# W1 and Wo loaded and split during the last batch of the first attention, and the opening units in another order

## What is computed

```python
x = x + _L0_attn_a_ref(_layernorm(x), ...)   # 8 heads, 128 wide, relative positions
x = x + _L0_ffn_ref(_layernorm(x), ...)      # 8 experts, all computed
x = x + _L0_attn_b_ref(_layernorm(x), ...)   # 16 heads, 8 wide, causal
x = x + _L0_ffn_ref(_layernorm(x), ...)
# in the FFN, for each expert e:
h = jnp.einsum('btd,hd->bth', x, W1[e]) + b1[e]
a, b = jnp.split(h, 2, axis=-1)
eo = jnp.einsum('bth,dh->btd', a * jax.nn.sigmoid(b), Wo) + bo
out = out + eo * comb[..., e:e + 1]          # comb: weights of the two best experts
```

## Time and profile before

| | us |
|---|---|
| median of 3 runs | 2921.26 |
| lowest and highest | 2916.53 and 2924.25 |
| the profiled execution | 2921.59 |
| its span | 2919.9 |
| TensorE busy | 2631.4 (90%) |
| VectorE busy | 2041.6 (70%) |
| ScalarE busy | 1656.7 (57%) |
| GpSimd busy | 355.0 (12%) |

### The profile page before, as it was taken

How to read it: one execution, slowest core, us unless ns; L and a number is a source line. 1 busy time by engine, 2 the same in 40 slices (tenths; PEclk the granted TensorE clock), 3 DMA queues, 4 the chain that set the end, 5 groups by cost and what they waited for, 6 DMA issues and landing times.

```text
span 2919.9 us, 45160 instructions
## 1 busy us (share of the span) xinstructions
PE 2631.4 (90%) x14496; PEld 2047.8 (70%) x14496; DVE 2041.6 (70%) x5231; ACT 1656.7 (57%) x3430; POOL 355.0 (12%) x782
## 2 busy tenths in 40 slices
PE   2899999999999999999997079988998989998998
PEld 1688788888888888888886067765555555554777
DVE  3576776767767677677664078869777776773887
ACT  2566666666666666666664044544666656565454
POOL 0000000000000000000000123321221221222344
PEclk9999999999999999999999589978999999999999
DMA  2655556566655566556663100000000000000000
GB/s 84 206 203 205 183 200 209 200 214 207 211 205 201 205 214 214 205 195 205 214 208 110 51 6 1 1 1 1 1 1 1 1 1 1 1 1 1 9 8 15
DMA packets 98467, 321.63 MB, mean 110 GB/s; under 512 B 11556, under 2 KB 25508, under 8 KB 98020
## 3 DMA queue, kind: packets, MB, share of 16 engines
q1 hardware_dynamic: 98234, 318.74, 31.9%
HBM read 158.53 MB, written 157.29 MB: 108 GB/s over the span
## 4 chain that ended last, share of the span: by engine, by line
PE 77%; DVE 11%; ACT 5%; SPq 3%; issue 3%; DMA 1%; POOL 0%; DVEq 0%; ACTq 0%; POOLq 0%
PE ps L238 7%; PE ps L240 7%; PE ps L239 7%; PE ps L608 7%; PE ps L583 5%; PE ps L582 5%; PE ps L721 4%; PE ps L759 4%; PE ps L621 4%; PE ps L623 4%; PE ps L622 4%; PE ps L653 4%; PE ps L741 4%; PE ps L654 4%; PE ps L655 4%
## 5 line engine op out<-in xcount | busy, mean ns | idle before, releaser
L874 ACT ACTIVATE a_Ph<-ps 128x512 fp32r<-128x512 f32 x512 | 305.9, 597 | 474.5 <-PE ps L608 474.4
L1177 DVE CUSTOM_DVE_ANT_0 a_sp<-ps,a_sp 128x1024 f32<-128x1024 f32 x256 | 313.3, 1224 | 184.8 <-PE ps L240 178.9
L952 ACT ACTIVATE r_P<-ps 128x512 f32<-128x512 f32 (+3 forms) x768 | 327.7, 491 | 187.5 <-PE ps L741 183.2
L1183 DVE TENSOR_TENSOR a_Pl<-ps,a_Ph 128x512 fp32r<-128x512 f32 x512 | 349.3, 682 | 10.1 <-ACT a_Ph L874 9.8
L582 PE MATMUL ps<-a_fa,a_ua 128*128 128x384 f32 (+2 forms) x960 | 327.2, 353 | 5.0 <-DMA a_ub<-a_ua 2.6
L903 ACT ACTIVATE r_y<-ps 128x256 f32<-128x256 f32 x512 | 194.4, 385 | 220.9 <-PE ps L655 215.0
L867 ACT ACTIVATE a_sp<-a_sp,a_nm 128x1024 f32<-128x1024 f32 x256 | 295.0, 1152 | 29.4 <-DVE a_nm L1177 29.3
L608 PE MATMUL ps<-ident,a_sp 128*128 128x128 f32 x2048 | 309.0, 273 | 0.0
L653 PE MATMUL ps<-r_Wh,p_xh 128*128 128x512 f32 x512 | 223.0, 436 | 92.1 <-DVE r_Wl L1212 44.6
L721 PE MATMUL ps<-r_K,r_Q 128*128 128x512 f32 (+3 forms) x768 | 281.9, 402 | 18.0 <-DVE r_mx L1339 12.6
L608 PEld LDWEIGHTS ps<-ident,a_sp 128*128 128x128 f32 x2048 | 250.7, 141 | 61.6 <-issue 0.4
(11 more groups left out here) (203 smaller groups left out, 5631.0 us busy)
## 6 DMA issues: line engine op xcount, KB each, us to landing
scr<-a_rt SPq DMA_DIRECT2D x256, 576.0 KB, 3.1
a_sp<-scr SPq DMA_DIRECT2D x256, 512.0 KB, 4.4
a_wc<-wsp SPq DMA_DIRECT2D x24, 512.0 KB, 5.5
wsp<-a_wc SPq DMA_DIRECT2D x8, 512.0 KB, 4.6
a_ub<-a_ua SPq DMA_DIRECT2D x64, 44.0 KB
x<-in_q SPq DMA_DIRECT2D x4, 512.0 KB, 15.9
wst<-in_w1t SPq DMA_DIRECT2D x8, 256.0 KB
out<-x SPq DMA_DIRECT2D x4, 512.0 KB, 3.2
```

The costliest lines, as they stand in the source:

```text
L952: e.activation(self.P[:, pt, off:512], ps[:, bank, off:512], ACT.Exp).then_inc(S["b_exp"], 1)
L1177: e.tensor_tensor_reduce(out=w, in0=ps[:, 2:4, :].rearrange("p a n -> p (a n)"), in1=w, scale=-1.0, scalar=3e38, op0=ALU.add, op1=ALU.min, ...
L1183: e.tensor_tensor(self.Pl[:, n % 3, :], ps[:, 4 + n % 2, :], self.Ph[:, n % 3, :].bitcast(F32), ALU.subtract).then_inc(S["p_lo"], 1)
```

## The change

It has these parts:

- W1's high part, half of its low part, and both parts of Wo get memory of their own (the other half of the low part takes the place of a tile of batches 0 and 2). Two staging buffers, `w1st` and `w1r`, hold a piece each.
- The units ("w1", 0) to ("w1", 8) stand at the end of steps 212, 216, ... 244 of plan_a. For piece k, SP issues its loads, GpSimd subtracts (now for all eight), ScalarE rounds and VectorE subtracts, all in this unit. The loads of piece k use buffer k % 2 and wait for the low part of piece k - 2. The last unit is Wo. What stood for this behind the first attention goes.
- SP issues the weights of head 0 ahead of x, and the loads of x for batches 1 to 3 are issued by ScalarE at the end of steps 4, 12 and 20 ("x_load").
- In the opening, the mix of head 0 comes first, its product in the middle of the layer norm, the rounding of the tables ("cut") and the rest of them ("table") apart, and the multiplication by the mask on GpSimd. Mix and prod of head 1 and x_bias go to the end of steps 0 and 1, the split of the gate weights ("route") to step 26.
- The mask of the second attention, `maskq`, is made by GpSimd behind the first attention, ahead of clearing K.
- TensorE no longer waits for first_attention_done ahead of the FFN; the banks' own semaphores stand for it.

```diff
-    p = splits(0)(0, 6) + [("x_bias", 0), ("table",), ("mix", 0), ("load", 1), ("prod", 0, 7)]
-    p += [("u", 0, 0, 2), ("u", 0, 1, 3), ("copy", 0), ("g", 0, 4)]
+    ln = splits(0)(0, 6)
+    p = [("mix", 0), ("load", 1)] + ln[:4] + [("prod", 0, 7)] + ln[4:] + [("cut",)]
+    p += [("u", 0, 0, 2), ("u", 0, 1, 3), ("copy", 0), ("table",), ("g", 0, 4)]
     for t in range(3):
         p += [("r", t, 0), ("r", t, 1), ("r", t, 2), ("rout", t)]
         if t:
             p.append(("rin", t - 1))
-    p += [("u", 1, 0, 5), ("u", 1, 1, 6), ("copy", 1), ("mix", 1), ("load", 2), ("prod", 1, 7)]
-    extra = {}
+    p += [("u", 1, 0, 5), ("u", 1, 1, 6), ("copy", 1)]
+    extra = {0: [("mix", 1), ("load", 2), ("x_bias", 0)], 1: [("prod", 1, 7)], 26: [("route",)]}
+    for b in range(1, B):
+        extra.setdefault(8 * b - 4, []).append(("x_load", b))
+    for k in range(E + 1):
+        extra.setdefault(64 * (B - 1) + 20 + 4 * k, []).append(("w1", k))
...
+        self.Wh, self.Wl = keep("w1h", [128, E, 512], F32R), keep("w1l", [128, E // 2, 512], F32R)
+        self.nat0 = keep("nat0", [128, 2, 8, 128], F32R)
+        late = self.nat0[:, :, :, :].rearrange("p a k n -> p (a k n)").rearrange("p (k n) -> p k n", n=512)
+        self.w1l = [self.Wl[:, k, :] for k in range(E // 2)] + [late[:, k, :] for k in range(E // 2)]
+        self.oh, self.ol = keep("woh", [128, 2, 128], F32R), keep("wol", [128, 2, 128], F32R)
...
+            self.w1st, self.w1r = sb("w1st", [128, 2, 512]), sb("w1r", [128, 2, 512])
...
+        weight_loads(0)
         e.dma_start(self.x[:, 0:8, :], xin[:, 0:8, :]).then_inc(self.d_x[0], 16)
-        weight_loads(0)
         e.dma_start(self.bias[:, :, :], dr["bias_a"].rearrange("d (a h) -> d a h", a=2)).then_inc(S["d_bias"], 16)
         e.dma_start(self.f0[:, :], bass.AP(dr["feat0"].tensor, 0, [[0, 128], [1, 96]])).then_inc(S["d_f0"], 16)
         e.dma_start(self.tmask[:, :], dr["tmask"]).then_inc(S["d_tmask"], 16)
         e.dma_start(self.raw[0], dr["feat_a"]).then_inc(S["d_tab"], 16)
         e.dma_start(self.raw[1], dr["feat_b"]).then_inc(S["d_tab"], 16)
-        for b in range(1, B):
...
+            elif u[0] == "w1":
+                k = u[1]
+                if k == 0:
+                    e.wait_ge(S["prod_mm"], H)
+                if k >= 2:
+                    e.wait_ge(S["w1_lo"], k - 1)
+                if k < E:
+                    e.dma_start(self.w1st[:, k % 2, :], w1[:, k, :]).then_inc(self.d_w1[k], 16)
+                    bottom_row(self.w1r[:, k % 2, :], "w1r", self.d_w1[k], slice(512 * k, 512 * k + 512))
+                else:
+                    e.dma_start(self.w1st[:, k % 2, 0:256].rearrange("p (k d) -> p k d", k=2),
+                                dr["wo_f"].rearrange("(k p) d -> p k d", p=128)).then_inc(S["d_wo"], 16)
...
-        w1 = dr["w1t"].rearrange("d (e h) -> d e h", e=E)
-        for k in range(E):
-            e.dma_start(self.w1st[:, k, :], w1[:, k, :]).then_inc(self.d_w1[k], 16)
-            bottom_row(self.w1r[:, k, :], "w1r", self.d_w1[k], slice(512 * k, 512 * k + 512))
-        e.dma_start(self.ost, dr["wo_f"].rearrange("(k p) d -> p k d", p=128)).then_inc(S["d_wo"], 16)
...
+        e.wait_ge(S["d_tmask"], 16)
+        for k, n in enumerate((128, NFB)):
+            e.wait_ge(S["tab_hi"], k + 1)
+            e.tensor_scalar(self.raw[k], self.raw[k], self.tmask[0:n, 2 * k + 1:2 * k + 2], None, ALU.mult).then_inc(
+                S["tab_cut"], 1)
+        for k in range(E):
+            st = self.w1st[:, k % 2, :]
+            e.wait_ge(self.d_w1[k], 48)
+            e.tensor_tensor(st, st, self.w1r[:, k % 2, :], ALU.subtract).then_inc(S["w1_sub"], 1)
+
         self.first_attention_done(e)
-        for k in range(0, E, 2):
-            e.wait_ge(self.d_w1[k], 48)
-            e.tensor_tensor(self.w1st[:, k, :], self.w1st[:, k, :], self.w1r[:, k, :], ALU.subtract).then_inc(S["w1_even"], 1)
+        e.memset(self.maskq[:, :], 0.0).then_inc(S["const"], 1)
+        e.wait_ge(S["const"], 4)
+        e.affine_select(out=self.maskq[:, 384:512], in_=self.maskq[:, 384:512], compare_op=ALU.is_ge, fill=NEG,
+                        **cond).then_inc(S["const"], 1)
         e.memset(self.K[:, :, :, :].bitcast(F32), 0.0).then_inc(S["b_kzero"], 1)
...
+        free[2] = free[3] = S["s_add"], NTI
+        free[4] = free[5] = S["p_lo"], 8 * NQ
         free[6] = S["o_lo"], NQ
 
     def tensor_ffn(self, e, f):
         S, ps, free = self.S, self.ps, self.bank_free
-        if f == 0:
-            self.first_attention_done(e)
...
+            elif u[0] == "x_load":
+                ns = slice(8 * u[1], 8 * u[1] + 8)
+                e.dma_start(self.x[:, ns, :], xin[:, ns, :]).then_inc(self.d_x[u[1]], 16)
+            elif u[0] == "route":
+                e.wait_ge(S["wg_diff"], 1)
+                e.activation(self.wgh[:, :], self.wgs[:, :], ACT.Copy).then_inc(S["wg_hi"], 1)
+            elif u[0] == "w1":
+                k = u[1]
+                if k < E:
+                    e.wait_ge(S["w1_sub"], k + 1)
+                    e.activation(self.Wh[:, k, :], self.w1st[:, k % 2, :], ACT.Copy).then_inc(S["w1_hi"], 1)
+                else:
+                    e.wait_ge(S["d_wo"], 16)
+                    e.activation(self.oh[:, :, :].rearrange("p k d -> p (k d)"), self.w1st[:, k % 2, 0:256],
+                                 ACT.Copy).then_inc(S["wo_hi"], 1)
+            elif u[0] == "cut":
...
+            elif u[0] == "route":
+                e.wait_ge(S["d_wg"], 16)
+                e.wait_ge(S["d_wgr"], 32)
+                e.tensor_tensor(self.wgs[:, :], self.wgs[:, :], self.wgr[:, :], ALU.subtract).then_inc(S["wg_diff"], 1)
+                e.wait_ge(S["wg_hi"], 1)
+                e.tensor_tensor(self.wgl[:, :], self.wgs[:, :], self.wgh[:, :].bitcast(F32), ALU.subtract).then_inc(S["wg_lo"], 1)
+            elif u[0] == "w1":
+                k = u[1]
+                if k == E // 2:
+                    e.wait_ge(S["pv_mm"], 128 * (B - 1))
+                if k < E:
+                    e.wait_ge(S["w1_hi"], k + 1)
+                    e.tensor_tensor(self.w1l[k], self.w1st[:, k % 2, :], self.Wh[:, k, :].bitcast(F32),
+                                    ALU.subtract).then_inc(S["w1_lo"], 1)
+                else:
+                    e.wait_ge(S["wo_hi"], 1)
+                    e.tensor_tensor(self.ol[:, :, :].rearrange("p k d -> p (k d)"), self.w1st[:, k % 2, 0:256],
+                                    self.oh[:, :, :].rearrange("p k d -> p (k d)").bitcast(F32),
+                                    ALU.subtract).then_inc(S["wo_lo"], 1)
             elif u[0] == "table":
-                e.wait_ge(S["d_tab"], 32)
-                e.wait_ge(S["d_tmask"], 16)
                 for k, n in enumerate((128, NFB)):
-                    e.wait_ge(S["tab_hi"], k + 1)
-                    self.step(e.tensor_scalar(self.raw[k], self.raw[k], self.tmask[0:n, 2 * k + 1:2 * k + 2], None, ALU.mult))
-                    e.wait_ge(S["dve_step"], self.steps)
+                    e.wait_ge(S["tab_cut"], k + 1)
...
-            for k in range(E):
-                if k % 2:
-                    e.wait_ge(self.d_w1[k], 48)
-                    e.tensor_tensor(self.w1st[:, k, :], self.w1st[:, k, :], self.w1r[:, k, :],
-                                    ALU.subtract).then_inc(S["w1_odd"], 1)
-                e.wait_ge(S["w1_hi"], k + 1)
-                e.tensor_tensor(self.Wl[:, k, :], self.w1st[:, k, :], self.Wh[:, k, :].bitcast(F32),
-                                ALU.subtract).then_inc(S["w1_lo"], 1)
-            e.wait_ge(S["wo_hi"], 1)
-            e.tensor_tensor(self.ol[:, :, :], self.ost, self.oh[:, :, :].bitcast(F32), ALU.subtract).then_inc(S["wo_lo"], 1)
...
-                    if m == 0:
-                        e.wait_ge(S["wo_lo"], 1)```

The order of the instructions, as the two programs give it. ScalarE before, behind the step-212 eviction of the last "r" (L859 evicts r, L874 makes a_Ph, L867 is the exponential):

```order
L874 ACTIVATE a_Ph<-ps 128x512 [waits pv_mm,t_mm]
L859 ACTIVATE a_rt<-ps 128x384 [waits r_mm]
L874 ACTIVATE a_Ph<-ps 128x512 [waits pv_mm,t_mm]
L859 ACTIVATE a_rt<-ps 128x384 [waits d_rout2,r_mm]
L867 ACTIVATE a_sp,a_ls<-a_sp,a_nm 128x1024 [waits s_add]
L874 ACTIVATE a_Ph<-ps 128x512 [waits pv_mm,t_mm]
```

65 lines of the change are left out of this document (23 added, 42 removed).

## The result

| us | before | after |
|---|---|---|
| median (4 runs of each) | 2920.03 | 2952.19 |
| lowest and highest | 2916.53 and 2924.25 | 2947.46 and 2957.38 |
| the profiled execution | 2921.59 | 2947.46 |
| its span | 2919.9 | 2945.7 |
| TensorE busy | 2631.4 | 2638.2 |

The change makes the kernel slower: 1.0112 times before's time, 95% interval 1.01 to 1.0125. The two profiles are 25.8 us apart and the medians 32: the profiled execution of after is the fastest of its four. What follows explains the 25.8.

What follows compares the result with a forecast made beforehand. TensorE was taken to have no slack in the first attention and to be nearly idle at its ends. Terms -88.7 (end), -32.3 (opening), +1.5 (x loads), +134.4 (pieces), +3.0 (Wo) gave +17.9 on 2921.6: 2939 us, range 2900 to 2960.

Steps and rivals of the forecast that it cites:

- opening, with the loads of x: Start of the kernel: reordered opening saves 32.3 us (bounds 28 to 37); loads of x on ScalarE's queue cost 1.5.
- eight pieces: W1 splits in the first attention: each piece stalls 16.8 us (bounds 13.9 and 19.5), +134.4 us for eight.
- Wo: Step 244: loading Wo costs 3 us, bounds 0 and 5.
- seam, up to the first merged tile: End of the first attention: FFN's first gate 91.3 us sooner, 0.6 and 2.0 given back, -88.7 us.
- order argument: W1 pieces: load and use stand in one step, so two buffers fetch nothing early and ScalarE waits.
- the price of GpSimd's multiplication: Opening: multiplying a table by the mask on GpSimd takes 1.7 us by its memset, 5.0 by its subtraction.
- The second term: Opening: mix and product 1 moved to steps 0 and 1, -7.5 us, with +3 given back (bounds 0 and 5).
- The term of 1.5: Steps 4, 12 and 20: loads of x may delay a rotated tile, +1.5 us, bounds 0 and 6.
- (a): W1 pieces: stalls cheaper, 15 us a piece, cancelling the gain, about 2925 us; chance 0.22.
- (b): W1 pieces: TensorE runs further ahead in the wait, 12.4 us a piece, 2904 us; chance 0.14.
- (d): Slow clock stays 6 us after each stall and x loads block ScalarE, 20 us a piece, 2965 us; chance 0.04.
- (c): W1 loads hidden if SP reaches a piece a step or more before ScalarE, 2802 us; chance 0.05.

Runs made afterwards that it cites:

- early2: The changed kernel with the loads of each piece of W1 issued two steps earlier: 2875.35 us, ratio 0.9859.
- early4: The changed kernel with the loads of each piece of W1 issued four steps earlier: 2869.73 us, ratio 0.9851.
- early4_split: The changed kernel with the loads four steps earlier and the repeated row split into transfers over 112 and 15 partitions: 2799.78 us, ratio 0.9596.
- poolq: The changed kernel with the pieces' loads issued by GpSimd on its own queue, two pieces ahead, repeated row not split: 2804.06 us, ratio 0.9608.
- row_on_act: The changed kernel with loads four steps early, the unsplit repeated row issued by ScalarE and the rest by SP: 2822.25 us, ratio 0.9677.

## Why the prediction was right in its sign, and where its terms were off

| term | forecast | measured in the profile |
|---|---|---|
| opening, with the loads of x | -32.3 + 1.5 | -28.9 |
| eight pieces | +134.4 | +146.3 |
| Wo | +3.0 | +4.7 |
| on the way to the last addition | 0 | +1.3 |
| seam, up to the first merged tile | -88.7 | -89.2 |
| behind it | 0 | -8.4 |
| sum | +17.9 | +25.8 |

The order argument held: with loads and uses in one step, two buffers fetched nothing ahead, ScalarE waited for GpSimd at each of eight pieces, and the gain at the seam was more than paid for. The forecast was 2939, the median 2952, the profiled execution 2947.5. That the sum came out as near as 7.9 us is in part luck: the terms up to the first merged tile were 16.3 us too low together, and 8.4 came back in stages for which the forecast had nothing.

- **The seam** was sized right in both its parts: the first gate 91.7 us sooner (forecast 91.3), 2.6 given back behind GpSimd's clearing of K (forecast 2.6).
- **The opening.** The first r was forecast at 38.0 with bounds 36.1 and 40.0, and ran at 41.03. The step that failed is the price of GpSimd's multiplication: 5.44 us a table, above the bound of 5.0 that was taken from a subtraction of two tiles, so a one-operand pass was no cheaper per element than a two-operand one. GpSimd's second table was ready at 38.3, which with a VectorE pass of 2.35 gives 40.65. Its effect on VectorE beside it, 5.80 for 2.35 us, was not in the sum at all, but fell mostly into that wait and cost only the last 0.3 us. By the Trainium skill ("GPSIMD Engine Reference", Engine selection) the tables would have been ready near 36.1; the measurement decides against it here. The second term was right: 7.3 us for mix and product 1 (forecast 7.5), and 3.3 given back on balance (forecast 3).
- **The loads of x** cost nothing visible: no distance is lost in after at steps 4, 12 and 20. In early2, early4, early4_split, poolq and row_on_act 0.8 to 1.1 us go at step 4, but step 4's minimum starts there (77.1 to 78.3 us) before the first of these loads is issued (78.4 to 79.6), so they are not its cause. The term of 1.5 should have been nothing. With step 4 and a clock of 0.83 between 84 and 94 us (1.00 in after), the same opening was worth 25.4 to 26.5 us at step 8 in these five kernels: 28.8 is not a constant of the change.
- **A piece** was forecast at 16.8 and cost 18.29, inside its bounds of 13.9 and 19.5. Two sub-steps were short. From the first issue to use it took 16.36 and not 14.7: by difference to the 13.42 of before, what stood ahead in SP's queue cost 2.9 us and not 1.3. And behind TensorE's idle time (15.47 us here, 15.3 on average) came 2.9 more and not 1.3: four microseconds at the lower clock, with a further 0.59 us of waiting for the low half of P, which stood behind the piece and the minimum on VectorE. The wait that stopped TensorE first was also another one than named: the r matmul waiting for ScalarE's eviction, not the pv matmul waiting for the low half.
- **Wo** cost 4.7 us, near its upper bound of 5.
- **Behind the first tile** the forecast had nothing, and 8.4 us came back. From the first merged tile to the end, before and then after:

```profile
1694.08:2919.87 1225.79, 1114.77 (x5879) 740.05 (x5877) 930.71 (x2862) 678.90 (x1549) 338.66 (x764) 0.94 0.01 3
...
1728.26:2945.72 1217.46, 1105.83 (x5876) 734.27 (x5876) 929.32 (x2861) 678.14 (x1547) 338.65 (x764) 0.95 0.01 3
```

TensorE does the same work in 8.9 us less busy time and is idle for as long as before, 111 us, so the gain goes with the granted clock. The change did not aim at it: the same stages took 1217 to 1223 us in the other kernels. That the clock is the cause is read from such rows only; no run tested it.

**The rivals.** (a) and (b) needed pieces of 15 us and less. (d) came nearest in its price, 20, though by the queue and the clock and not by ScalarE's blocked issue: ScalarE's issues of x took about 0.4 us each. (c) said 2802 if the loads were hidden; early4_split hides them and takes 2799.8. Its terms met the forecast as a sum, not singly: the opening was 5.4 us worse, and 4.8 us came back behind the first merged tile. What its condition lacked is that asking a step or more ahead is not enough: early4 does so and takes 2869.7, since the repeated row then holds up the tiles of the same queue. The prediction took 13.4 us from issue to use from a row and never asked why 254 KB should take that long when 512 KB land in 4.4. That question would have led to the transfer that cost before 68 us all along.

## What to carry to other kernels

Two buffers hide a load only if the issuing engine reaches the issue before the users reach the use; where all engines walk one list, give the load a place of its own, some steps ahead. Then look at what stands behind it in its queue, for a slow transfer moved off one path stalls another. And compare each transfer's landing time with others by bytes: one that is several times too slow is worth mending before anything is moved around it.

## What the runs showed of the hardware beyond that

- The repeated row over 127 partitions kept a DMA share of 0.07 and moved 25 GB/s (after, 1313 to 1322 us). Its 254 KB took 13.0 us from issue to use on SP's queue, some 20 on ScalarE's with SP's tiles beside it, and they landed in 4.3 us on GpSimd's. Split over 112 and 15 partitions, with its piece and last row, it was usable 6.1 us after the first issue on SP's.
- With that row in flight, the issue of the next small transfer (L367 in after, L368 in early4) held SP for 4.0 to 6.1 us; with the split it took 0.24.
- GpSimd's multiplication of 128 x 2048 by one value per partition took 5.44 us, VectorE's 1.28. VectorE's pass with two inputs from memory took 5.80 us beside it and 2.34 to 2.35 alone.
